# A three-stage decoder layer on one core: context logits by two 64-row halves of the PE array, the bias of Q added by PE, key maxima taken later

## The chip, the cores and the metric

The kernel runs on one core of one Trainium2 chip. The metric is device time in microseconds of one execution, as the median of several; lower is better. TensorE (PE) multiplies, VectorE (DVE), ScalarE (ACT) and GpSimd (POOL) work on what it leaves in PSUM and in SBUF, and SyncE (SP) issues most of the DMAs. Each engine takes its instructions in program order and waits on semaphores.

## The reference

The input is x of 4 batches of 1024 tokens of 256 numbers. Three layers follow one another, each with a residual sum and a layer norm. Shortened:

```python
q, k, v = x @ Wq.T + bq, x @ Wk.T + bk, x @ Wv.T + bv      # 16 heads of 16
q = softmax(q, axis=-1)                                    # over the 16 numbers of a head
k = softmax(k, axis=-2)                                    # over the 1024 tokens of a batch
state = einsum('bhnd,bhne->bhde', k, v)
x = layernorm(x + (layernorm(q @ state) * g + b) @ Wo.T + bo)
# context attention: 8 heads of 32, 77 keys, keys and values straight from the context
logits = einsum('bhqd,bhkd->bhqk', x * 32 ** -0.5, keys) + b0 - 1e30 * (1 - mask)
x = layernorm(x + softmax(logits) @ values)
# mixture of experts: 8 experts of 256 -> 1024 -> 256, the 4 best of each token
x = layernorm(x + sum over 4 experts of gate * (gelu(x @ up[e]) @ down[e]))
```

## The kernel before

The 4096 tokens are cut into 32 tiles of 128 tokens, eight to a batch. The program is a software pipeline of 52 steps, written out by hand for each engine. In step s the first part of one tile is done (`first_tile(s)`: Q, K and V), and parts of up to six older tiles (`chain_tile(s, d)`, called c0 to c6). A ninth step at the end of each batch (`closing(s)`) takes the largest K of every column, shifts and exponentiates the eight K tiles, and builds the linear attention's state. Steps 0 to 37 hold the front of the pipeline together with the splitting of the experts' weights into two float16 halves, which passes through DMA, ACT, POOL and DVE in 16 pieces. Steps 38 to 51 hold the last tiles mixed with the first expert tiles. After them only the experts are left, and a last norm.

The steps of Q, K and V. PE multiplies the turned input tile by K's and V's weights into bank 0 of a 1024-wide `big` PSUM tile (L1838) and by Q's weights into its bank 1 (L1840); as float32 each product of 128 rows is two passes. ACT copies K and V out (L1020, L1021), behind the copies of the turned tiles `x1T` and `xinT`. DVE (`take_qkv`) adds the bias to Q into SBUF (L1150, which frees Q's bank), takes the largest of each head of 16 (L1153), waits for ACT's copy of K and joins it to the running maximum `kmx` (L1159), and takes the head's maximum off Q (L1161). Then in the same step DVE divides the heads' outputs of another tile (`out_of_heads`, L1412 and L1414), takes their moments, norms the tile c4, makes the first residual sum and its moments (L1424), takes the logits' extremes (L1432, L1438), and does parts of the routing. POOL takes the square root of each variance (L827, L829), adds the constants to the residual (L835) and issues the scatters of the routing records (L851).

The context logits. `kbd` holds the context keys of a batch, negated, as a block matrix: for each half c of the 256 columns, 128 rows by 4 heads of 77 keys, in which a head's 32 rows alone are not zero. It is made by DVE (`key_blocks`, L1143) from the turned keys and the selector `hsel`. For every tile PE (`context_logits`) makes two products of 128 rows by 308 columns in float32 (L1730), one for each half c and each into its own bank, and after each adds the mask by one product of 128 rows by 308 columns in bfloat16 (L1731): `one16` has ones in row 0 alone, and row 0 of `mbf` holds the mask for 4 heads. POOL makes this row once a batch (`mask_row`, L839 and four instructions L844 of one partition each). ACT exponentiates the eight heads one by one (L992), PE turns them (L1719), and multiplies by the values (L1741).

The order in PE's queue within a step of the front: turn Z, turn Q, Q/K/V products, turn X1, turn the next input, heads' outputs (L1699), output projection (L1709), a column sum of a weight piece (L1861), turn the probabilities (L1719), context logits, turn X2, the values' products (L1741) and the router's (L1753). In the mixed steps these are set between the experts' products (`up_products` L1801, `down_products` L1820), one chunk of four after another.

Of the kernel before, what the change touches and what calls it, by code (L numbers as in the profile page):

```python
# [9 lines left out]
I32 = mybir.dt.int32  # L10
# [13 lines left out]
XPC = P // XD  # L24
KEYS = 77
# [29 lines left out]
IDENT_MADE, ONES_MADE = 2, 3  # L55
# [298 lines left out]
def layer(nc, k, rows, acc, slots, x, ctx, mask, Wq, bq, Wk, bk, Wv, bv, Wo, bo, ln_g, ln_b, xb, router, up, down, out):  # L354

    st, places = ExitStack(), ExitStack()
    with st:
# [29 lines left out]
        kbd = sb("kbd", [P, CC, XPC, KEYS])  # L387
        hsel = sb("hsel", [P, XPC])
# [4 lines left out]
        mint = sb("mint", [1, KEYS], I32)  # L393
        mrow = sb("mrow", [1, KEYS])
# [52 lines left out]
        inv = sb("inv", [P, 2 * EXP])  # L447

# [10 lines left out]
        V_extra = extra[:, C:C + CC * (P + 1)].rearrange("p (c m) -> p c m", c=CC)  # L459

# [43 lines left out]
        big_ready, qkv_taken = sem("big_ready"), sem("qkv_taken")  # L504
# [116 lines left out]
        def _(sp):  # L621
# [140 lines left out]
        def _(pool):  # L762
# [11 lines left out]
            done(pool.memset(ones[:, :], 1.0))  # L774
            done(pool.memset(V[:, :, :, P:P + 1], 1.0))
# [5 lines left out]
            done(pool.memset(one16[:, :], 0.0))  # L781
            done(pool.memset(one16[0:1, :], 1.0))
            done(pool.memset(mbf[:, :, :], 0.0))
# [8 lines left out]

            for tile, heads, d in ((hsel, XPC, XD), (bsel, HPC, LD)):
                done(pool.memset(tile[:, :], -1.0 if tile is hsel else 1.0))
                done(pool.affine_select(out=tile[:, :], in_=tile[:, :], compare_op=ALU.is_ge, fill=0.0,
                                        base=0, pattern=[[-d, heads]], channel_multiplier=1))
                done(pool.affine_select(out=tile[:, :], in_=tile[:, :], compare_op=ALU.is_ge, fill=0.0,
                                        base=d - 1, pattern=[[d, heads]], channel_multiplier=-1))
            for c in range(CC):
                done(pool.tensor_copy(state[:, c, P:P + HPC], bsel[:, :]))  # L800
# [36 lines left out]
            def mask_row(b):  # L837
                pool.wait_ge(mask_loaded, 16 * (b + 1))
# [96 lines left out]
        def _(act):  # L935
# [50 lines left out]
            def exp_logits(g):  # L986
# [4 lines left out]
                for h_ in range(XH):  # L991
                    ins = act.activation(pr[:, h_, :], logits[:, h_, :], ACT.Exp, scale=-1.0, bias=xmb[:, g % 2, h_:h_ + 1])  # L992
# [94 lines left out]
        def _(dve):  # L1087
# [3 lines left out]

            dve.wait_ge(setup_loaded2, 16 * 8)
            dve.wait_ge(consts, ONES_MADE)

            for c in range(CC):
                dve.tensor_scalar(kdiag[:, c, :], ones[:, :], gb[:, 1, c:c + 1], None, ALU.mult).then_inc(lnbb_ready, 1)
            for c in range(CC):
# [42 lines left out]
            def key_blocks(b):  # L1140
                for c in range(CC):
                    dve.wait_ge(end_ready, END_COUNT[(TB + 1) * b + TB + 2])
                    dve.tensor_tensor(kbd[:, c, :, :], turned_keys(b, c).unsqueeze(1).to_broadcast([P, XPC, KEYS]),  # L1143
                                      hsel[:, :].unsqueeze(2).to_broadcast([P, XPC, KEYS]), ALU.mult).then_inc(kt_taken, 1)

            def take_qkv(g):
                i = g % TB
                src = big_bank(("qkv", g))
                dve.wait_ge(big_ready, BIG["qkv", g] + 1)
                dve.tensor_tensor(query_tile(g), src[:, 2 * C:3 * C], bias[:, 0:C], ALU.add).then_inc(qkv_taken, 1)  # L1150
                q3 = query_tile(g).rearrange("p (h d) -> p h d", h=LH)
                dve.wait_ge(qkv_taken, g + 1)
                dve.tensor_reduce(qm[:, g % 2, :], q3, AX_X, ALU.max).then_inc(qm_ready, 1)  # L1153
# [6 lines left out]
                dve.wait_ge(qm_ready, g + 1)  # L1160
                dve.tensor_tensor(q3, q3, qm[:, g % 2, :].unsqueeze(2).to_broadcast([P, LH, LD]), ALU.subtract).then_inc(qs_ready, 1)  # L1161
# [339 lines left out]
            for s in range(MIX0):  # L1501
# [18 lines left out]
                if c1 is not None:  # L1520
# [3 lines left out]
                    moments(1, c1)  # L1524
                if piece is not None:
                    scale(piece)
# [97 lines left out]
        def _(pe):  # L1624
# [31 lines left out]
            def big_emptied(key):  # L1656
                kind, g = key
                if kind == "qkv":
                    pe.wait_ge(qkv_taken, g + 1)
# [62 lines left out]
            def context_logits(g):  # L1722
# [101 lines left out]
            for s in range(MIX0):  # L1824
# [133 lines left out]
```

## Time and profile before

| what | value |
|---|---|
| median of 3 runs | 1242.4 us (1237.84 to 1242.64) |
| the profiled execution | 1242.11 us, its span 1240.4 us |
| mean granted TensorE clock of its span | 0.938 |
| PE, DVE, POOL, ACT busy | 1080.2, 742.2, 641.0, 528.0 us |
| front of the pipeline | to about 398 us |
| mixed steps | about 398 to 567 us |
| experts alone | about 567 to 1206 us |
| last norm and stores | about 1206 us to the end |

The page gives busy times and the chain of waits: from the last instruction back to what released it, and so on to the start. A shorter instruction brings the end nearer only if it stands on this chain, and only by as much as the next chain allows. A group of instructions on one line can be partly on it. Views by windows give the stages, the timeline gives the pace of an engine. Durations of matmuls overlap in the records, so the pace is read from start to start.

### The profile page before, as it was taken

What the parts mean: (1) busy time and instruction counts of PE and PEld (TensorE: products, weight loads), DVE (VectorE), ACT (ScalarE), POOL (GpSimd) and SP (SyncE); (2) the same over time, 40 slices, a digit from 0 to 9 for tenths busy, and PEclk for the clock granted to TensorE, in tenths of its full rate; (3) what the DMA queues carried; (4) which work ended last, traced back from release to release, by engine and by line L of the source; (5) the groups of instructions that cost most, each with busy time, mean ns of one, the idle gap of its engine ahead of it and who ended that gap; (6) DMA issues with size and microseconds to landing.
All of it is one profiled execution on the core that took longest, in us unless ns stands there. A gap on an engine that the chain in (4) does not pass through costs nothing.

```text
span 1240.4 us, 27263 instructions
## 1 busy us (share of the span) xinstructions
PE 1080.2 (87%) x8576; PEld 910.7 (73%) x8576; DVE 742.2 (60%) x1813; ACT 528.0 (43%) x1148; POOL 641.0 (52%) x739
## 2 busy tenths in 40 slices
PE   6668898798864998989989999999999999999960
PEld 3345676576644887878878888888888888888750
DVE  2568988888875665765674544444444444444326
ACT  2765665544543445554433333333333333333214
POOL 3003332657665566766777555555555555554324
PEclk9878998998876998999999999999999999999985
DMA  4553222213022323334344544655444445553336
GB/s 126 167 163 96 84 81 80 51 44 84 27 63 57 81 46 67 62 66 83 47 81 74 88 78 78 78 79 78 78 79 78 75 75 75 76 75 58 63 55 247
DMA packets 159969, 100.63 MB, mean 81 GB/s; under 512 B 106956, under 2 KB 151168, under 8 KB 159840
## 3 DMA queue, kind: packets, MB, share of 16 engines
q1 hardware_dynamic: 129824, 63.21, 20.1%
q0 software_dynamic: 30016, 35.68, 19.3%
q8 instruction: 83, 1.36, 0.5%
q14 instruction: 46, 0.38, 0.1%
HBM read 49.55 MB, written 31.59 MB: 65 GB/s over the span
## 4 chain that ended last, share of the span: by engine, by line
PE 67%; DVE 12%; ACT 8%; issue 4%; DMA 4%; POOL 4%; SPq 1%; DVEq 0%; ACTq 0%; POOLq 0%
PE big L1801 28%; PE big L1820 15%; PE trans L1820 11%; PE big L1838 2%; POOL slot_records L851 2%; ACT pr L992 1%; PE big L1730 1%; PE small L1709 1%; PE trans L1632 1%; PE small L1741 1%; PE small L1887 1%; DMA w_down<-in_L_ffn_down_w_dram 1%; DVE stat L1130 1%; PE big L1840 1%; ACT L992 1%
## 5 line engine op out<-in xcount | busy, mean ns | idle before, releaser
L1801 PE MATMUL big<-xgT,w_up 128*128 128x256 f16 (+1 forms) x3456 | 410.7, 268 | 10.7 <-ACT h L976 6.2
L976 ACT ACTIVATE h<-big,up_scale 128x512 f32<-128x512 f32 x270 | 185.6, 687 | 438.0 <-PE big L1801 429.2
L1801 PEld LDWEIGHTS big<-xgT,w_up 128*128 x3456 | 326.3, 99 | 54.3 <-issue 14.3
L881 POOL DMA_INDIRECT token_sums<-y,rec x135 | 223.4, 1654 | 246.6 <-ACT y L984 216.8
L1404 DVE TENSOR_SCALAR hh<-h,h_scale 128x512 f16<-128x512 f32 x270 | 133.1, 493 | 346.7 <-ACT h L976 346.1
L1820 PE MATMUL big<-w_down,hh 128*128 x1312 | 223.7, 272 | 2.5 <-DVE hl L1406 2.2
L1406 DVE SCALAR_TENSOR_TENSOR hl<-h,h_scale,hh 128x512 f16<-128x512 f32 x270 | 203.3, 753 | 9.7
L1820 PE MATMUL big<-w_down,hl 128*128 x656 | 178.8, 273 | 0.0
L866 POOL DMA_INDIRECT xg<-token_rows,rec x135 | 136.5, 1011 | 51.3 <-issue 39.0
L851 POOL DMA_INDIRECT slot_records<-recs,posi x128 | 133.2, 1040 | 34.8 <-issue 34.8
L1820 PE MATMUL trans<-w_down,hh 128*128 x848 | 144.6, 273 | 2.3 <-DVE hl L1406 2.3
L827 POOL TENSOR_SCALAR ve<-mv 128x1 f32<-128x1 f32 x96 | 27.3, 284 | 229.3 <-DVE mv L1134 228.7
L1820 PEld LDWEIGHTS big<-w_down,hh 128*128 128x128 f16 x1312 | 128.2, 98 | 20.8 <-issue 4.5
L1820 PE MATMUL trans<-w_down,hl 128*128 x424 | 115.6, 273 | 0.0
L1820 PEld LDWEIGHTS trans<-w_down,hh 128*128 128x128 f16 x848 | 82.9, 98 | 12.6 <-issue 2.6
L1838 PE MATMUL big<-wqkv_XA,xinT 128*128 128x512 f32 x128 | 72.1, 693 | 1.4 <-ACT xinT L944 1.4
L1820 PEld LDWEIGHTS big<-w_down,hl 128*128 128x128 f16 x656 | 64.1, 98 | 7.3
L829 POOL TENSOR_TENSOR rstd<-ve,nhalf 128x1 f32<-128x1 f32 x96 | 60.4, 629 | 8.0
L992 ACT ACTIVATE pr<-big,xmb 128x77 f32<-128x77 f32 x256 | 58.8, 348 | 11.3 <-DVE xmb L1438 11.1
L951 ACT ACTIVATE pT<-trans 128x512 f32<-128x512 f32 x64 | 24.5, 434 | 60.2 <-PE trans L1719 59.4
L1709 PE MATMUL small<-woT,zT 128*128 128x256 f32 x128 | 40.6, 447 | 10.9 <-DVE L L1470 4.2
L1730 PE MATMUL big<-kbd,x1T 128*128 128x308 f32 x128 | 45.9, 449 | 0.0
(261 smaller groups left out, 1416.1 us busy)
## 6 DMA issues: line engine op xcount, KB each, us to landing
w_down<-in_L_ffn_up_w_dram SPq DMA_DIRECT2D x8, 1024.0 KB, 5.0
w_down<-in_L_ffn_down_w_dram SPq DMA_DIRECT2D x7, 1024.0 KB, 5.7
wqkv_XA<-in_x_dram SPq DMA_DIRECT2D x32, 128.0 KB, 2.7
XRES<-in_x_dram SPq DMA_DIRECT2D x32, 128.0 KB
token_sums<-X SPq DMA_DIRECT2D x32, 128.0 KB, 1.7
token_rows<-XR SPq DMA_DIRECT2D x32, 128.0 KB, 1.7
sums<-token_sums SPq DMA_DIRECT2D x8, 512.0 KB, 6.5
out_dram<-sums SPq DMA_DIRECT2D x8, 512.0 KB, 2.6
```

The source lines that it names most:

```text
L829: pool.tensor_tensor(rstd[:, kind, at:at + 1], ve[:, kind, at:at + 1], nhalf[:, 0:1], ALU.pow).then_inc(rstd_ready[kind], 1)
L851: pool.indirect_dma_start(slots, bass.IndirectOffsetOnAxis(ap=posi[:, half, e:e + 1], axis=0), recs[:, half, e // TOPK, e % TOPK, :], None ...
L866: pool.indirect_dma_start(xg[:, t % 2, j, :], None, rows[0:EARLY_BATCHES * N, :] if t < EARLY else rows, bass.IndirectOffsetOnAxis(ap=rec[ ...
L881: pool.indirect_dma_start(acc[0:EARLY_BATCHES * N, :] if t < EARLY else acc, bass.IndirectOffsetOnAxis(ap=rec[:, t % RING, j, 0:1], axis=0 ...
L976: act.activation(h[:, i % H_RING, :], psu[up_bank(i)], ACT.Gelu_apprx_tanh, scale=k["up_scale"][:, t:t + 1]).then_inc(gelu_ready, 1)
L992: ins = act.activation(pr[:, h_, :], logits[:, h_, :], ACT.Exp, scale=-1.0, bias=xmb[:, g % 2, h_:h_ + 1])
L1404: dve.tensor_scalar(hh[:, i % HALF_RING, :], h[:, i % H_RING, :], k["h_scale"][:, t:t + 1], None, ALU.mult).then_inc(hh_ready, 1)
L1406: dve.scalar_tensor_tensor(out=hl[:, i % HALF_RING, :], in0=h[:, i % H_RING, :], scalar=k["h_scale"][:, t:t + 1], in1=hh[:, i % HALF_RING, :],
L1730: pe.matmul(dst, x1T[:, c, :], kbd[:, c, :, :].rearrange("p h k -> p (h k)"), start=True, stop=False)
L1801: ins = pe.matmul(psu[up_bank(i)][:, j * size(t):(j + 1) * size(t)], w[:, ws, c, m:m + P], xgT[:, t % 2, xs * CC + c, 0:size(t)], start=(n ...
L1820: ins = pe.matmul(ytile(t)[:, j, :], (hh, hl)[hs][:, i % HALF_RING, at:at + P], w[:, ws, c, :], start=(c == 0 and j == 0 and hs == 0 and w ...
L1838: pe.matmul(dst[:, 0:2 * C], xT[:, c, :], wqkv[:, c, C:3 * C], start=(c == 0), stop=(c == CC - 1))
```

## The change

- `kbd` keeps 2 heads of 77 keys for each half c in place of 4: rows 0 to 63 hold two heads and rows 64 to 127 the other two, in the same columns. `hsel` gets two more columns for it.
- PE makes the logits in six products of 64 rows: two in bfloat16 for the mask (308 columns each), which now come first, and four in float32 of 154 columns. Products of rows 0 to 63 go into one bank and those of rows 64 to 127 into the other. The order of heads in PSUM changes, and ACT writes them back in the old order.
- `one16` has ones everywhere; `mint`, `mrow` and `mbf` have 128 rows, of which 0 and 64 carry the mask and the others zeros. POOL makes `mbf` in one instruction in place of four; SP loads the mask twice.
- Q's bias is added by PE: one bfloat16 product of 128 rows by 256 columns before the products of Q, with the bias as a sum of three bfloat16 rows. DVE makes these rows at the start in eight instructions, before it takes the `cv` sums.
- DVE takes the heads' maxima and the differences of Q straight from PSUM; the addition is gone, and Q's bank is free after the differences.
- The running maximum of K is taken later in the step, after the moments of the first residual sum (`take_key`).

```diff
-        kbd = sb("kbd", [P, CC, XPC, KEYS])
+        kbd = sb("kbd", [P, CC, HALF_HEADS, KEYS])
...
+                else:
+                    sp.wait_ge(consts, CONST_STEPS)
                 sp.dma_start(ctx_sb[:, :], ctx[b, :, 0:C]).then_inc(ctx_loaded, 16)
-                sp.dma_start(mint[:, :], mask[b:b + 1, :]).then_inc(mask_loaded, 16)
+                for a in range(2):
+                    sp.dma_start(mint[a * HALF_ROWS:a * HALF_ROWS + 1, :], mask[b:b + 1, :]).then_inc(mask_loaded, 16)
...
-                for h in range(XPC):
-                    ins = pool.tensor_scalar(mbf[0:1, h, :], mrow[:, :], -MASKED, None, ALU.mult)
-                ins.then_inc(mask_ready, 1)
+                pool.tensor_scalar(mbf[:, :, :], mrow[:, :].unsqueeze(1).to_broadcast([P, XPC, KEYS]), -MASKED, None, ALU.mult).then_inc(mask_ready, 1)
...
+            def query_bias_rows():
+
+                high, low = XR[:, 0, 0:C].bitcast(BF16), XR[:, 1, 0:C].bitcast(BF16)
+                left, rest = X2[:, 0, :], X2[:, 1, :]
+                dve.memset(bq_rows[:, :], 0.0).then_inc(bq_step, 1)
+                dve.tensor_copy(high, bias[:, 0:C]).then_inc(bq_step, 1)
+                dve.wait_ge(bq_step, 2)
+                dve.tensor_tensor(left, bias[:, 0:C], high, ALU.subtract).then_inc(bq_step, 1)
+                dve.wait_ge(bq_step, 3)
+                dve.tensor_copy(low, left).then_inc(bq_step, 1)
+                dve.wait_ge(bq_step, 4)
+                dve.tensor_tensor(rest, left, low, ALU.subtract).then_inc(bq_step, 1)
+                dve.wait_ge(bq_step, 5)
+                dve.tensor_copy(bq_rows[0:1, :], bias[0:1, 0:C]).then_inc(bq_ready, 1)
+                dve.tensor_copy(bq_rows[32:33, :], left[32:33, :]).then_inc(bq_ready, 1)
+                dve.tensor_copy(bq_rows[64:65, :], rest[64:65, :]).then_inc(bq_ready, 1)
...
-                src = big_bank(("qkv", g))
+                src = big_bank(("qkv", g))[:, 2 * C:3 * C].rearrange("p (h d) -> p h d", h=LH)
                 dve.wait_ge(big_ready, BIG["qkv", g] + 1)
-                dve.tensor_tensor(query_tile(g), src[:, 2 * C:3 * C], bias[:, 0:C], ALU.add).then_inc(qkv_taken, 1)
-                q3 = query_tile(g).rearrange("p (h d) -> p h d", h=LH)
-                dve.wait_ge(qkv_taken, g + 1)
-                dve.tensor_reduce(qm[:, g % 2, :], q3, AX_X, ALU.max).then_inc(qm_ready, 1)
+                dve.tensor_reduce(qm[:, g % 2, :], src, AX_X, ALU.max).then_inc(qm_ready, 1)
+                dve.wait_ge(qm_ready, g + 1)
+                dve.tensor_tensor(query_tile(g).rearrange("p (h d) -> p h d", h=LH), src,
+                                  qm[:, g % 2, :].unsqueeze(2).to_broadcast([P, LH, LD]), ALU.subtract).then_inc(qs_ready, 1)
+
+            def take_key(g):
+                i = g % TB
                 dve.wait_ge(kv_ready, 2 * g + 1)
...
-                dve.wait_ge(qm_ready, g + 1)
-                dve.tensor_tensor(q3, q3, qm[:, g % 2, :].unsqueeze(2).to_broadcast([P, LH, LD]), ALU.subtract).then_inc(qs_ready, 1)
...
                     moments(1, c1)
+                if a is not None:
+                    take_key(a)
...
                 logits = big_into(("lg", g))
+                for a in range(2):
+                    at = LOGIT0 + a * XPC * KEYS
+                    pe.matmul(logits[:, at:at + XPC * KEYS], one16[row_half(a), :], mbf[row_half(a), :, :].rearrange("p h k -> p (h k)"),
+                              start=True, stop=False, skip_group_check=True)
                 for c in range(CC):
-                    dst = logits[:, LOGIT0 + c * XPC * KEYS:LOGIT0 + (c + 1) * XPC * KEYS]
-                    pe.matmul(dst, x1T[:, c, :], kbd[:, c, :, :].rearrange("p h k -> p (h k)"), start=True, stop=False)
-                    ins = pe.matmul(dst, one16[:, :], mbf[:, :, :].rearrange("p h k -> p (h k)"), start=False, stop=True)
+                    for a in range(2):
+                        at = LOGIT0 + (CC * a + c) * HALF_HEADS * KEYS
+                        ins = pe.matmul(logits[:, at:at + HALF_HEADS * KEYS], x1T[row_half(a), c, :], kbd[row_half(a), c, :, :].rearrange("p h k -> p (h k)"),
+                                        start=False, stop=(c == CC - 1), skip_group_check=True)
...
+                    if a == 0:
+                        pe.wait_ge(consts, ONE16_MADE)
+                        pe.wait_ge(bq_ready, 3)
+                    pe.matmul(dst[:, 2 * C:3 * C], one16[:, :], bq_rows[:, :], start=True, stop=False)
                     for c in range(CC):
-                        ins = pe.matmul(dst[:, 2 * C:3 * C], xT[:, c, :], wqkv[:, c, 0:C], start=(c == 0), stop=(c == CC - 1))
+                        ins = pe.matmul(dst[:, 2 * C:3 * C], xT[:, c, :], wqkv[:, c, 0:C], start=False, stop=(c == CC - 1))
```

## Rows read from the trace of the kernel before

**Rows 1.** The page: the engines' busy times, the chain's lines.
```profile
PE 1080.2 (87%) x8576; PEld 910.7 (73%) x8576; DVE 742.2 (60%) x1813; ACT 528.0 (43%) x1148; POOL 641.0 (52%) x739
...
PE big L1801 28%; PE big L1820 15%; PE trans L1820 11%; PE big L1838 2%; POOL slot_records L851 2%; ACT pr L992 1%; PE big L1730 1%; PE small L1709 1%; PE trans L1632 1%; PE small L1741 1%; PE small L1887 1%; DMA w_down<-in_L_ffn_down_w_dram 1%; DVE stat L1130 1%; PE big L1840 1%; ACT L992 1%
```

**Rows 2.** Windows by stage: from:to, length, busy time per engine, granted clock.
```profile
85.00:180.00 95.00, 81.78 (x445) 61.50 (x444) 79.44 (x225) 61.15 (x168) 32.69 (x63) 0.93 0.30 95
...
340.00:398.00 58.00, 30.72 (x170) 25.48 (x167) 37.87 (x121) 21.09 (x64) 35.87 (x46) 0.72 0.20 53
398.00:567.00 169.00, 152.56 (x1237) 132.11 (x1237) 110.79 (x286) 87.73 (x199) 110.86 (x126) 0.95 0.34 66
```

**Rows 3.** The chain, 268 to 345 us: start, length, engine, line.
```profile
283.04 0.43 POOL mbf L844
...
285.18 0.24 POOL ve L827
...
290.11 3.41 PE big L1838 x4
293.52 1.17 PE big L1840 x4
...
328.99 1.03 PE big L1730 x2
```

**Rows 4.** The same chain, one step that waits for K.
```profile
310.88 1.72 PE big L1838 x4
312.59 0.86 PE big L1840 x4
...
314.26 0.40 ACT K L1020
314.68 0.43 DVE kmx L1159
315.11 0.33 DVE Q L1161
315.44 0.18 DVE rden L1412
```

**Rows 5.** The same chain, one step in which DVE itself is late.
```profile
304.22 0.34 DVE Q L1150
...
304.92 0.41 DVE kmx L1159
305.34 0.34 DVE Q L1161
305.67 0.18 DVE rden L1412
```

**Rows 6.** The chain, 460 to 500 us: one mixed step.
```profile
477.34 1.31 PE big L1801 x12
478.65 0.52 PE big L1730 x2
479.17 0.13 PE big L1731
479.31 0.52 PE big L1730 x2
479.82 0.13 PE big L1731
...
481.26 1.06 PE small L1741 x10
```

**Rows 7.** Timeline of PE, 465 to 500 us: the record's own length.
```profile
478.49 0.68 PE L1730 MATMUL big<-kbd,x1T 128*128 128x308 f32 x2
```

**Rows 8.** Timeline of the start: DVE before and at the second cv sum.
```profile
13.37 0.48 DVE L1096 TENSOR_SCALAR kdiag<-ones,gb 128x128 f32<-128x128 f32 x2 [13.37 <-DMA rw<-in_L_ffn_router_w_dram]
...
16.08 0.29 DVE L1099 TENSOR_TENSOR cvec<-small,cvec 128x128 f32<-128x128 f32 x1 [0.56 <-PE small L1685]
```

**Rows 9.** Groups by line and shape, 30 to 490 us: a copy on DVE.
```profile
L1156 DVE COPY kmx<-K 128x256 f32<-128x256 f32 x2 | 0.6, 288 | 0.0
```

More of the change, by code:

```diff
@@ L24 @@
 XPC = P // XD
+HALF_ROWS, HALF_HEADS = P // 2, XPC // 2
 KEYS = 77
@@ L54 @@
 CONST_STEPS = 32 + 3 * FCH + TOPK + EXP
-IDENT_MADE, ONES_MADE = 2, 3
+IDENT_MADE, ONES_MADE, ONE16_MADE = 2, 3, 4
 PIECES = 4
@@ L386, in layer @@
         x2T = sb("x2T", [P, CC, P])
-        kbd = sb("kbd", [P, CC, XPC, KEYS])
-        hsel = sb("hsel", [P, XPC])
+        kbd = sb("kbd", [P, CC, HALF_HEADS, KEYS])
+        hsel = sb("hsel", [P, XPC + HALF_HEADS])
         bsel = sb("bsel", [P, HPC])
@@ L392, in layer @@
         vx = sb("vx", [P, FCH, SPAN_MAX, XD + 1])
-        mint = sb("mint", [1, KEYS], I32)
-        mrow = sb("mrow", [1, KEYS])
+        mint = sb("mint", [P, KEYS], I32)
+        mrow = sb("mrow", [P, KEYS])
         mbf = sb("mbf", [P, XPC, KEYS], BF16)
@@ L447, in layer @@
         inv = sb("inv", [P, 2 * EXP])
+        bq_rows = sb("bq_rows", [P, C], BF16)
         trans = [ps(f"trans{i}", [P, 4, P]) for i in range(2)]
@@ L459, in layer, with row_half, head_at @@
         V_extra = extra[:, C:C + CC * (P + 1)].rearrange("p (c m) -> p c m", c=CC)
+        def row_half(a):
+            return slice(a * HALF_ROWS, (a + 1) * HALF_ROWS)
+        def head_at(n):
+            a, c, j = n // XPC, n // HALF_HEADS % CC, n % HALF_HEADS
+            return XPC * c + HALF_HEADS * a + j
         def key_tile(g):
@@ L503, in layer @@
         rt_taken, pos_taken, early_taken = sem("rt_taken"), sem("pos_taken"), sem("early_taken")
-        big_ready, qkv_taken = sem("big_ready"), sem("qkv_taken")
+        big_ready, bq_step, bq_ready = sem("big_ready"), sem("bq_step"), sem("bq_ready")
         lnbb_ready, woT_gained, woT_centred = sem("lnbb_ready"), sem("woT_gained"), sem("woT_centred")
@@ L774, in _ @@
             done(pool.memset(ones[:, :], 1.0))
+            done(pool.memset(one16[:, :], 1.0))
             done(pool.memset(V[:, :, :, P:P + 1], 1.0))
@@ L780, in _ @@
             done(pool.memset(nhalf[:, :], -0.5))
-            done(pool.memset(one16[:, :], 0.0))
-            done(pool.memset(one16[0:1, :], 1.0))
-            done(pool.memset(mbf[:, :, :], 0.0))
+            done(pool.memset(mint[:, :], 1))
             done(pool.memset(vx[:, :, :, :], 0.0))
@@ L791, in _ @@
                                         pattern=[[KEYS, h1 - h0]], channel_multiplier=-1))
-            for tile, heads, d in ((hsel, XPC, XD), (bsel, HPC, LD)):
-                done(pool.memset(tile[:, :], -1.0 if tile is hsel else 1.0))
-                done(pool.affine_select(out=tile[:, :], in_=tile[:, :], compare_op=ALU.is_ge, fill=0.0,
+            for tile, heads, d, value in ((hsel[:, 0:XPC], XPC, XD, -1.0), (bsel[:, :], HPC, LD, 1.0)):
+                done(pool.memset(tile, value))
+                done(pool.affine_select(out=tile, in_=tile, compare_op=ALU.is_ge, fill=0.0,
                                         base=0, pattern=[[-d, heads]], channel_multiplier=1))
-                done(pool.affine_select(out=tile[:, :], in_=tile[:, :], compare_op=ALU.is_ge, fill=0.0,
+                done(pool.affine_select(out=tile, in_=tile, compare_op=ALU.is_ge, fill=0.0,
                                         base=d - 1, pattern=[[d, heads]], channel_multiplier=-1))
+            done(pool.tensor_tensor(hsel[:, XPC:XPC + HALF_HEADS], hsel[:, 0:HALF_HEADS], hsel[:, HALF_HEADS:XPC], ALU.add))
             for c in range(CC):
@@ L837, in mask_row @@
             def mask_row(b):
-                pool.wait_ge(mask_loaded, 16 * (b + 1))
+                pool.wait_ge(mask_loaded, 16 * 2 * (b + 1))
                 pool.tensor_scalar(mrow[:, :], mint[:, :], -1.0, 1.0, ALU.mult, ALU.add).then_inc(mask_step, 1)
@@ L990, in exp_logits @@
                 logits = big_bank(("lg", g))[:, LOGIT0:LOGIT0 + XH * KEYS].rearrange("p (h k) -> p h k", h=XH)
-                for h_ in range(XH):
-                    ins = act.activation(pr[:, h_, :], logits[:, h_, :], ACT.Exp, scale=-1.0, bias=xmb[:, g % 2, h_:h_ + 1])
+                for n in range(XH):
+                    ins = act.activation(pr[:, head_at(n), :], logits[:, n, :], ACT.Exp, scale=-1.0, bias=xmb[:, g % 2, n:n + 1])
                 ins.then_inc(p_ready, 1)
@@ L1096, in _ @@
                 dve.tensor_scalar(kdiag[:, c, :], ones[:, :], gb[:, 1, c:c + 1], None, ALU.mult).then_inc(lnbb_ready, 1)
+            query_bias_rows()
             for c in range(CC):
@@ L1658, in big_emptied @@
                 if kind == "qkv":
-                    pe.wait_ge(qkv_taken, g + 1)
+                    pe.wait_ge(qs_ready, g + 1)
                     pe.wait_ge(kv_ready, 2 * (g + 1))
```

4 lines of the change are left out of this document (2 added, 2 removed).

## Prediction, made before the change was run

> **What bounds the kernel now.** I read the page first [rows 1]. PE is busy for 87% of the span and most of the chain is PE's, but nearly all of that is experts' work on L1801 and L1820, which the change leaves alone. The windows say where there is something to win [rows 2]. In the front of the pipeline (85 to 180 us) PE is busy 81.8 of 95 us and DVE 79.4: neither is the bound alone, and the chain passes from one to the other. From 340 to 398 us PE is half idle. In the mixed steps (398 to 567 us) PE is busy 152.6 of 169 us. Then I followed the chain itself through the front and the mixed steps, and counted in which steps the touched lines stand on it.
>
> The Q/K/V products L1838 stand on it in 12 of 32 tiles (2.1% of the span, about 26 us, as the page has it [rows 1]); three of the 12 run at the lower clock, 3.41 us in place of 1.72 [rows 3, 4]. The running maximum of K stands on it in 19 tiles. In 14 of them it comes behind ACT's copy of K [rows 4]: Q's products end at 313.46 and DVE divides the heads' outputs (rden) at 315.44, 2.0 us later, though nothing in rden needs K. In five DVE is late by itself, and the four operations follow one another without a gap [rows 5]. The context logits stand on the chain in 7 tiles of the front and in all 8 of the mixed steps [rows 6]. The row of the mask stands on it once [rows 3].
>
> **The change part by part.** Minus is a gain.
>
> *Maxima of Q and K.* In a step that waits for K, DVE goes on after Q's products with the reduction (the record of each of the four operations is about 0.42 us) and the difference, some 0.85 us in all by the spacing of [rows 5]: reduction 0.45, difference 0.33, small gaps. The heads' outputs, which PE makes behind two turns, are ready about 1.1 us after Q's products. So rden starts 1.1 us after them in place of 1.7 to 2.0: 0.6 to 0.9 earlier. The maximum of K is still to be taken, 0.35 us, but later; where the chain stays on DVE up to there this is given back. I take 0.55 a tile between 0.25 and 0.85: 14 tiles, -7.7 us (-3.5 to -11.9). In the five steps of [rows 5] one operation of about 0.33 us goes: 304.22 to 305.67 is 1.45, and becomes 1.1 with K's maximum counted: -1.7 us. Q's bank is freed by the second operation as before, counted from PE's end 0.4 us later; the next product into it comes a step later (some 10 us), so this costs nothing. The K maximum of the last tile of a batch, for which PE's turn in the closing step waits, moves about 2 us back within its own step, before left products of the next, and is hidden by them.
>
> *Bias by PE.* One product of 256 columns in bfloat16 is added to each tile. Twelve float16 products of 256 columns take 1.31 us [rows 6], so it is 0.11 us, or 0.22 at the lower clock. On the chain in 12 tiles, three of them slow: +1.6 us. In the other tiles PE isn't late.
>
> *Context logits.* Before: 478.65 to 479.95, 1.30 us [rows 6]: four passes of 0.26 in float32 and two masks of 0.13. After: eight float32 passes of 154 columns and two masks. If each pair of halves runs together, that is 8 x 0.13 / 2 + 0.13 = 0.64 us. If none does, it is 8 x 0.13 + 2 x 0.13 = 1.30. The trace has no product of 64 rows and no change of the rows used, so its cost is bounded: 0, or the tail of a product that is normally hidden, 0.68 - 0.52 = 0.16 us [rows 6, 7], once going in and once coming out. The bounds are 0.64 and 1.62. Between them a row decides: ten float32 passes of at most 99 columns take 1.06 us (L1741 [rows 6]), 0.106 each although their columns need but 0.08, so a pass doesn't get shorter than about 0.106, the load of its weights. Eight such and two masks at half price are 0.98; with some loss at the changes I take 1.10, a gain of 0.2 (0.66 gained to 0.32 lost). With 15 tiles on the chain: -3.0 us (-9.9 to +4.8).
>
> What speaks against this part stands in the Trainium skill too. TensorEngine Tiling (Array Packing), Key Properties, says that changing the tiling mode drains TensorE; this kernel would change it twice a tile. No row here shows a drain; by it the value goes to the upper end. TensorE: Matmul & The Clock Gate, LDWEIGHTS (loading the stationary operand), has the load take as long as its columns at 1.2 GHz whatever the rows, an estimate of 8 x 107 ns = 0.85 us for the eight; the pace of L1741 agrees.
>
> *Mask, keys, setup.* On POOL four instructions (283.04 to 285.18, 2.14 us [rows 3]) become one of 128 x 308. Its price isn't in the trace: it lies between 0.4 (one of the four) and about 1.2 (by its columns from the 0.8 us of a 128 x 256 addition there); I take 0.7, and -1.4 us, for it is on the chain once. `key_blocks` halves its columns: two operations of 0.47 become about 0.3; on the chain in one batch, -0.3. SP issues one more small DMA a batch (0.4 us), with the tile's stores behind it in SP's queue; nothing on the chain waits for these; if something did, +1.6. At the start DVE makes the bias rows in eight operations: about 0.29 for each of five copies [rows 9], 0.42 for each of two differences, a memset, in all some 2.6 us from 13.9 to 16.5, ahead of the two cv sums, of which DVE took the second at 16.08 [rows 8]. Both now come after 16.5, so the first qkv product comes about 0.7 later; since step 0 of DVE is shorter after that, the weights' first load comes 0.6 later. +0.6 (0 to +1.3).
>
> Sum: -7.7 - 1.7 + 1.6 - 3.0 - 1.4 - 0.3 + 0.6 = -11.9 us. What is late next takes part of it: ACT, whose copies of K, X1 and the input keep their times, and POOL, which is busy 35.9 of the 58 us between 340 and 398, more than PE [rows 2], and whose scatters there only move with their start. I take 2 us off: -10. The profiled execution took 1242.1 and the median is 1242.4, so they may be taken as one: 1232 us.
>
> **The rivals.** *The halves don't run together* (the change doesn't do what it says): 1.60 a tile with the changes of rows, +4.5 in place of -3.0: 1239.5. For it: both passes of a half follow each other in program order, so neighbours are of different halves only every second time. Against it: they go into different banks and rows. *The halves run together fully*: 0.64 a tile, -9.9 in place of -3.0: 1225. Against it: the pace of 0.106 a pass. *The wait for K only moves*: the heads' outputs aren't ready earlier, or K's maximum comes to a point where DVE is just as late. Then of 9.4 us about 3 is left: 1238.5. For it: PE's turn of X1 and the input stand before the heads' outputs, and DVE is 84% busy in the front. *Slower: PE's clock falls in more of the front's steps.* It stands at 0.93 there [rows 2] with 86% of PE busy. A slow step costs about 1.7 us in L1838, 0.5 to 0.8 in L1840, 1.3 in the logits (two passes take 1.03 in place of 0.52 [rows 3, 6]) and 0.8 in L1741, about 4.5 in all where PE is on the chain. Two more such steps than now eat the whole gain, four give 1232 + 18 = 1250. For it: work is taken off PE where the clock already falls at times. Against it: it is less than a tenth of PE's work in a step.
>
> **How the numbers follow.** The sum as told has 0.40, with a range of its own of 1227 to 1237; no concurrency 0.20, full concurrency 0.15, the wait only moves 0.15, the clock 0.10. The range of 1222 to 1246 takes in the first four and their bounds, and leaves out most of the fifth. A difference under about 0.5% (6.2 us) can't be told from none here. Below 1236.2 fall nine tenths of the first case, all of the third, a fifth of the second and the fourth: 0.58. Above 1248.6 falls most of the fifth: 0.08. Between them 0.34.
>
> **What would show it.** Right: rden about 1.1 us behind the end of L1840 in the steps of the second kind of chain; the six logits' products from first start to the next product's start in 1.0 to 1.2 us; expert work of the last stage unchanged and the first mixed step starting 8 to 9 us earlier than at about 398; a mixed step shorter by 0.2 us. Wrong: the logits over 1.3 us; an ACT or POOL wait in front of the same steps with the same length of the front; a granted clock below 0.9 between 85 and 340 us. If DVE is still on the chain at K's maximum, in its new place, the first term was too large.

## The result, and the profile after

The changed kernel takes 1221.6 us (median of 4 runs, 1219.7 to 1223.5) against 1240.1 of the kernel before beside it; the ratio is 0.9856, with a 95% interval of 0.9831 to 0.9882. That is 18 us faster, where 10 were forecast, and just outside the range. (The forecast of 1232 started from 1242.4 us; 2.3 of the 10.4 us between it and the measured 1221.6 are the lower starting point of this comparison, the other 8 are the gain.) Two more comparisons on other chips gave 0.9837 (0.981 to 0.9864) and 0.985 (0.9825 to 0.9874), so 18 to 20 us. The runs of the kernel before spread more (1231.5 to 1243.8 in 29 runs on one chip) than those of the changed one, and its profiled execution of 1242.1 lies at the slow end. So what a part is worth is told from the timed ratios, in microseconds of 1238, and the traces tell where.

The page of the changed kernel, the busy times and the chain by engine (the busy times of before are in [rows 1]):

```profile
PE 1064.8 (87%) x8736; PEld 898.6 (74%) x8736; DVE 729.8 (60%) x1789; ACT 527.4 (43%) x1148; POOL 637.1 (52%) x727
...
PE 63%; DVE 15%; ACT 7%; POOL 6%; issue 5%; DMA 4%; SPq 1%; DVEq 0%; ACTq 0%; POOLq 0%
```

The chain by engine of the kernel before:

```profile
PE 67%; DVE 12%; ACT 8%; issue 4%; DMA 4%; POOL 4%; SPq 1%; DVEq 0%; ACTq 0%; POOLq 0%
```

PE's share of the whole chain is down from 67% to 63% and DVE's is up from 12% to 15%. The windows, in the same columns as [rows 2], the later ones shifted with the stages:

```profile
85.00:180.00 95.00, 83.16 (x520) 63.26 (x519) 82.80 (x236) 66.27 (x185) 32.54 (x66) 0.94 0.32 101
...
340.00:380.00 40.00, 21.13 (x115) 18.21 (x115) 21.57 (x69) 16.13 (x44) 26.97 (x31) 0.67 0.16 37
380.00:550.00 170.00, 153.81 (x1334) 134.57 (x1333) 111.50 (x286) 88.11 (x199) 113.63 (x125) 0.97 0.36 68
```

DVE is busy 82.8 of the 95 us from 85 to 180, against 79.4 in [rows 2], although each tile has one operation less: more tiles fall into the same 95 us. Where the time went can be read from the first starts of the last Q/K/V product, of the first expert product and of the last logits, before and after. PE's timelines, before:

```profile
334.30 1.88 PE L1838 MATMUL big<-wqkv_XA,xinT 128*128 128x512 f32 x4
...
550.38 0.68 PE L1730 MATMUL big<-kbd,x1T 128*128 128x308 f32 x2
```

and after:

```profile
315.63 1.88 PE L1875 MATMUL big<-wqkv_XA,xinT 128*128 128x512 f32 x4
...
379.69 2.53 PE L1838 MATMUL big<-xgT,w_up 128*128 128x256 f16 x11 [3.27 <-DMA xgT<-xg]
...
526.76 0.31 PE L1762 MATMUL big<-mbf,one 64*128 64x308 bf16 x2
```

In these two executions 18.7 us are won by the end of the front (334.3 to 315.6), the same 18.7 are there when the experts begin (398.4 in the chain of before, 379.7 after), and 4.9 more come in the mixed steps (550.4 to 526.8 is 23.6). So most of it lies in the front and the rest in the mixed steps. (This pair overstates the front, for the trace of before is of a slow execution; three traces of the changed kernel have the first expert product at 378.8, 379.7 and 380.6.)

A piece of the chain after, from 85 to 150 us (start, length, engine and line). It stands on DVE from one tile's Q to the next, where before it passed through PE and ACT [rows 4]:

```profile
125.08 0.32 DVE qm L1179
125.42 0.42 DVE Q L1181
125.84 0.17 DVE rden L1442
126.04 0.44 DVE Z L1444
...
127.44 0.41 DVE X L1454
...
128.43 0.41 DVE kmx L1191
...
134.72 0.32 DVE qm L1179
```

How often DVE waited for the Q products of PE is in the waits between 17 and 340 us (who waited for whom: us in total, times, longest), before and after:

```profile
DVE Q L1150 <- PE big L1840: 16.0, 12, 3.6
```

```profile
DVE qm L1179 <- PE big L1881: 13.8, 9, 3.5
```

In the kernel before DVE waited for them in 12 of 32 tiles. In the other 20 it came to them from earlier work of its own, in 17 of these over 0.8 us after PE had finished them, so DVE was late already. (Some of that work had itself waited for ACT's pieces of the weights.) In the changed kernel DVE came without a wait in 23 tiles.

### The profile page after: what moved, and what is told of

The parts are those of the page before. It is cut to its first block, busy times and chain, and to the rows that moved or that the text cites. A ratio compares the mean times of both kernels' runs of the same rounds, so it can differ in the third digit from the quotient of the medians.

```text
span 1217.7 us, 27552 instructions
## 1 busy us (share of the span) xinstructions
PE 1064.8 (87%) x8736; PEld 898.6 (74%) x8736; DVE 729.8 (60%) x1789; ACT 527.4 (43%) x1148; POOL 637.1 (52%) x727
## 3 DMA queue, kind: packets, MB, share of 16 engines
q0 software_dynamic: 30016, 35.68, 20.2%
## 4 chain that ended last, share of the span: by engine, by line
PE 63%; DVE 15%; ACT 7%; POOL 6%; issue 5%; DMA 4%; SPq 1%; DVEq 0%; ACTq 0%; POOLq 0%
PE big L1838 29%; PE big L1857 15%; PE trans L1857 11%; POOL slot_records L862 3%; DMA w_down<-in_L_ffn_down_w_dram 1%; DVE stat L1159 1%; ACT pr L1003 1%; PE small L1741 1%; DVE w_down L1155 1%; DVE xm L1462 1%; PE small L1778 1%; ACT L1003 1%; PE trans L1664 1%; ACT L987 1%; PE big L1875 1%
## 5 line engine op out<-in xcount | busy, mean ns | idle before, releaser
L1838 PE MATMUL big<-xgT,w_up 128*128 128x256 f16 (+1 forms) x3456 | 411.2, 268 | 11.2 <-ACT h L987 6.2
L1838 PEld LDWEIGHTS big<-xgT,w_up 128*128 x3456 | 326.5, 99 | 55.2 <-issue 14.7
L1875 PE MATMUL big<-wqkv_XA,xinT 128*128 128x512 f32 x128 | 69.6, 671 | 1.4 <-ACT xinT L955 1.4
L1664 PE MATMUL trans<-ident,X 128*128 128x128 f32 x128 | 27.7, 300 | 22.5 <-DVE X L1167 11.1
```

What stands on the lines that cost most here:

```text
L1838: ins = pe.matmul(psu[up_bank(i)][:, j * size(t):(j + 1) * size(t)], w[:, ws, c, m:m + P], xgT[:, t % 2, xs * CC + c, 0:size(t)], start=(n ...
```

## Experiments: the three parts, alone and in pairs

The change falls into the logits in halves (L, with the mask in one instruction), the bias on PE (B) and the later maximum of K (K). All six mixtures were timed. The edits take parts of the diff back; the core of each:

```diff
# without L: products of 128 rows, kbd of 4 heads, mask row by four instructions
-                for c in range(CC):
-                    for a in range(2):
-                        at = LOGIT0 + (CC * a + c) * HALF_HEADS * KEYS
...
+                    pe.matmul(dst, x1T[:, c, :], kbd[:, c, :, :].rearrange("p h k -> p (h k)"), start=True, stop=False)
+                    ins = pe.matmul(dst, one16[:, :], mbf[:, :, :].rearrange("p h k -> p (h k)"), start=False, stop=True)
# without B: DVE adds the bias
-                    pe.matmul(dst[:, 2 * C:3 * C], one16[:, :], bq_rows[:, :], start=True, stop=False)
+                dve.tensor_tensor(query_tile(g), big_bank(("qkv", g))[:, 2 * C:3 * C], bias[:, 0:C], ALU.add).then_inc(qkv_taken, 1)
# without K: the maximum between the heads' maxima and the differences
+                take_key(g)
                 dve.wait_ge(qm_ready, g + 1)
```

L alone (l_only):

> Only the logits by 64-row halves (with the mask row in one POOL instruction); Q's bias and the maximum of K stay where they were. In the changed kernel a tile's logits take 0.76 us on PE in place of 1.30. Theory A (the parts are worth what their places on the chain say and add up): 15 tiles x 0.54 = 8.1 us, and 1 us for the mask: about 9 us faster than before. Theory B (PE and DVE share a loop; while DVE still waits for K behind PE, a shorter PE shows up fully in the mixed steps alone): 8 x 0.54 = 4.3 us there, and 2 to 3 in the front: 6 to 7 us.

K alone (k_only):

> Only the running maximum of K is taken later; the bias stays on DVE and the logits are of 128 rows. Theory A: in the 14 tiles in which DVE waited for ACT's copy of K the wait goes, 0.25 to 0.5 us each net of the maximum itself: 4 to 7 us faster. Theory B (the wait for K was what tied DVE to PE and ACT, with ACT's exponentials ahead of the copy): 8 to 12 us faster, most of it between 90 and 200 us.

B alone (b_only):

> Only Q's bias goes to PE; K's maximum stays between the heads' maxima and the differences. (The bias rows lie in memory of scale tables that are free by then, for there is no room beside the wide key blocks.) Theory A: in the steps in which DVE is late one operation of 0.33 us goes (5 tiles, 1.7 us), on PE 0.11 is added on 12 tiles (1.6 us), and the eight operations at the start cost up to 0.6: 0 to 1 us slower or no change. Theory B (DVE's load is what counts everywhere): 32 x 0.33 = 10 us faster at most, 4 or more.

B and K (b_k):

> Bias on PE and K's maximum later, logits of 128 rows as before. Theory A: the sum of the two alone, 4 to 8 us faster. Theory B: more than the sum, 10 to 12 us, since only with both is DVE free to go on right behind PE; then the logits' halves add 7 to 9 on top.

L and K (l_k):

> The changed kernel with Q's bias back on DVE: K's maximum late and the logits in halves stay. Theory C: the bias addition costs DVE 0.33 to 0.4 in most of the 32 tiles: 7 to 11 us slower than the changed kernel. Theory A: 1 us faster to 1 us slower, since PE's product and the rows at the start go away too.

L and B (l_b):

> The changed kernel with K's maximum back between the heads' maxima and the differences. If DVE's work were all that counts, nothing would change, since the same operation is only moved. If the wait for ACT's copy of K is a cost of its own (12.0 us of such waits in the trace with the bias on PE alone, against 5.4 before), it is 8 to 14 us slower than the changed kernel.

The whole change again, beside them (after_again):

> The changed kernel once more, beside runs of the kernel before on the same chip as the three kernels sent with it. Every theory: 16 to 20 us faster than before.

| parts | median us | ratio to before (95%) | us |
|---|---|---|---|
| L | 1235.0 | 0.9981 (0.996 to 1.0002) | -2.4 |
| K | 1229.4 | 0.9947 (0.9927 to 0.9967) | -6.6 |
| B | 1233.7 | 0.9975 (0.9951 to 0.9999) | -3.1 |
| B, K | 1222.0 | 0.9878 (0.985 to 0.9906) | -15.1 |
| L, K | 1227.9 | 0.9906 (0.9877 to 0.9934) | -11.6 |
| L, B | 1233.0 | 0.9949 (0.9928 to 0.9969) | -6.3 |
| all | 1219.3 | 0.9837 (0.981 to 0.9864) | -20.2 |

B and K alone make 9.7, together 15.1. The 5.4 us between them are beyond the spread (the means of the four kernels' runs on that chip give 4.5, give or take 3). B is worth 3.1 by itself and 8.5 once K's maximum is out of the way (8.6 beside L and K, on another chip); K is worth 6.6 by itself and 12 beside B, and 12 to 14 beside L and B. The waits of DVE between 17 and 340 us say why (the columns as above). Before, then with B alone, then with all:

```profile
DVE kmx L1159 <- ACT K L1020: 5.4, 10, 1.6
```

```profile
DVE kmx L1195 <- ACT K L1034: 12.0, 18, 2.1
```

```profile
DVE kmx L1191 <- ACT K L1031: 0.9, 2, 0.6
```

Take the addition off DVE and it comes sooner to the maximum of K, where it waits for ACT's copy: 12.0 us in 18 tiles in place of 5.4 in 10. What was taken off is given back as a wait. With the maximum moved the wait is gone. L and B together show the same wait without the move, 11.8 us in 18 tiles. Theory A of the expectations holds for K alone (6.6 in 4 to 7). B alone, at 3.1, lies between the two theories. For the pair more than the sum was right, as theory B has it, and 15.1 is more than its 10 to 12.

L is the surprise of the other kind: 2.4 us alone, where both theories had 6 to 9 and the interval reaches from a gain of 5 to no change; 3.2 on top of B, 5.0 on top of K, and between 3 and 5 on top of both.

The mixed steps alone can account for that. From the first expert product to the product behind the last logits it is 153.3 us before, 153.2, 150.4 and 151.2 with B, with K and with both, and 147.8 to 148.3 in the six traces that have L (L, L and B, L and K, and three of the whole change): 2 to 5.5 us less. In the front nothing of L is left over.

One thing goes with it that the experiments did not separate. Each kernel with L ran at a lower granted clock, averaged over the span and all its runs, than its partner without: 0.937 for L against 0.942 before, 0.937 for L and B against 0.945 for B, 0.941 for L and K against 0.946 for K, 0.942 for all against 0.949 for B and K. Among the 29 runs of the kernel before on one chip a clock lower by 0.001 goes with a time longer by 0.9 us. If the same held between kernels, the lower clock would take back 4 to 7 us of what L gives, an estimate that no run tests.

## Experiments: do the halves run together?

Edits of the changed kernel: all six products over 128 rows (each then takes the rows of both halves, so that kernel doesn't compute the layer); and the order of the four float32 products. The first edit, its lines shortened:

```diff
-                    pe.matmul(logits[:, at:at + XPC * KEYS], one16[row_half(a), :], mbf[row_half(a), :, :]
+                    pe.matmul(logits[:, at:at + XPC * KEYS], one16[:, :], mbf[:, :, :]
...
-  x1T[row_half(a), c, :], kbd[row_half(a), c, :, :]
+  x1T[:, c, :], kbd[:, c, :, :]
```

```diff
-                for c in range(CC):
-                    for a in range(2):
+                for a in range(2):
+                    for c in range(CC):
```

> The changed kernel with every one of the six logits' products over all 128 rows, the number of products, their columns and their banks as they are (the logits are wrong, as each product takes both halves' rows; the masks are added twice). Halves at once: the six take 0.76 us in the changed kernel and 8 x 0.13 + 2 x 0.13 = 1.30 here, 0.54 more in each of the 8 mixed steps, and 4 to 6 us in all. If the 0.76 came from fewer columns or from the masks standing first, the six take 0.76 here too and the time is the same.

> The changed kernel with the four float32 products in the order half 0, half 0, half 1, half 1. If only neighbours in the queue run together, two of eight passes overlap and the six products take about 1.1 us in place of 0.76, 2 to 4 us slower in all. If PE looks further ahead, nothing changes.

PE's timelines between 445 and 500 us, from the twelve expert products ahead to the next one behind; a record of several is from the first start to the last modelled end. All over 128 rows:

```profile
458.52 1.47 PE L1838 MATMUL big<-xgT,w_up 128*128 128x256 f16 x12
459.83 0.42 PE L1762 MATMUL big<-mbf,one 128*128 128x308 bf16 x2
460.09 1.21 PE L1767 MATMUL big<-kbd,x1T 128*128 128x154 f32 x8
461.14 0.38 PE L1857 MATMUL big<-w_down,hh 128*128 x2
```

The halves, in the order of the change:

```profile
455.20 1.47 PE L1838 MATMUL big<-xgT,w_up 128*128 128x256 f16 x12
456.61 0.31 PE L1762 MATMUL big<-mbf,one 64*128 64x308 bf16 x2
456.75 0.69 PE L1767 MATMUL big<-kbd,x1T 64*128 64x154 f32 x8
457.37 0.39 PE L1857 MATMUL big<-w_down,hh 128*128 x2
457.60 0.27 PE L1857 MATMUL big<-w_down,hl 128*128 x1
```

The halves one after the other:

```profile
456.26 0.30 PE L1762 MATMUL big<-mbf,one 64*128 64x308 bf16 x2
456.40 0.80 PE L1767 MATMUL big<-kbd,x1T 64*128 64x154 f32 x8
457.12 0.39 PE L1857 MATMUL big<-w_down,hh 128*128 x2
```

From the first mask product to the next expert product it is 1.31, 0.76 and 0.86 us. The same products over all rows take what the old ones took (1.30, [rows 6]), so the 0.55 comes from the halves running together and not from fewer columns or from the order of the masks.

Not all of it is a gain. The twelve expert products ahead take 1.31 us to the next start when that product has 128 rows (459.83 - 458.52, and 1.31 in [rows 6]), and 1.41 when it has 64 (456.61 - 455.20; 1.40 or 1.41 in the four such steps between 430 and 500 us). So going over to 64 rows costs 0.10 us. Coming back costs about 0.01: 0.23 us from 457.37 to 457.60, where the kernel before has 0.22. With the entry a tile's logits cost PE 0.86 us in place of 1.31, a gain of 0.45, or 3.6 us in the 8 mixed steps.

With one half after the other it costs 0.10 more, less than the 0.3 expected of strict neighbours. In time, rows128 has a ratio of 0.9863 (1222.2 us) and order_by_half 0.9856 (1220.7), against 0.9837 and 0.985 of the changed kernel on other chips. For rows128 that is 2 to 3 us, hardly beyond the spread (4 to 6 were expected), and for the order nothing that can be measured. The mixed stretch of rows128 takes 153.3 us, as before the change, and its first expert product starts at 379.8 us, as in the changed kernel. So the longer logits cost the front nothing that shows. Here too the clock stands beside it: rows128 ran at 0.946 on average, the changed kernel at 0.942, so it isn't shown whether the front would gain from shorter logits at an equal clock.

## Experiments: which engine sets the front's pace?

Doses of work were put on one engine. On DVE, at the early place, with a semaphore of its own:

```diff
+                dve.tensor_reduce(qm[:, g % 2, :], src, AX_X, ALU.max).then_inc(twice, 1)
+                dve.wait_ge(twice, g + 1)
                 dve.tensor_reduce(qm[:, g % 2, :], src, AX_X, ALU.max).then_inc(qm_ready, 1)
```

> The changed kernel, with the reduction of the heads' maxima done twice for every tile of Q (some 0.42 us and a wait more on DVE, 32 times, at the place where the bias addition stood). Theory C (in the front DVE's own work sets the pace almost everywhere once K's wait is gone): 32 x 0.42 x 0.7 or more, 9 to 13 us slower than the changed kernel. Theory A (as in the forecast, DVE is late in few steps): 2 to 5 us slower.

> The kernel before, with the same reduction done twice ahead of the maximum of K. Theory C: there part of the steps hide it behind ACT's copy of K, so it costs less than in the changed kernel, 3 to 7 us. If it costs as much as in the changed kernel (9 to 13), DVE set the pace before as well, and the forecast's five tiles were miscounted.

The same on `kmx` at the late place, and the early one again beside it:

```diff
+                    dve.tensor_tensor(kmx[:, :], kmx[:, :], key_tile(g), ALU.max).then_inc(twice, 1)
+                    dve.wait_ge(twice, g - g // TB)
                     dve.tensor_tensor(kmx[:, :], kmx[:, :], key_tile(g), ALU.max).then_inc(kmx_ready, 1)
```

> The changed kernel with the running maximum of K done twice, in its late place behind the moments of the first residual sum: 28 operations of 0.35 to 0.42 us and a wait more on DVE. Theory D (what counts is where on DVE an operation stands: ahead of the heads' outputs it delays every engine, behind the moments only DVE's own tail): 2 to 5 us slower than the changed kernel, as the mirror image of the 3.6 us that taking them out gave. Theory C (DVE's load alone): 28/32 of the doubled reduction, 9 to 10 us slower.

> The changed kernel with the reduction of the heads' maxima done twice, beside the doubled maximum of K on the same chip. Both theories: 9 to 12 us slower than the changed kernel, that is 7 to 10 us faster than the kernel before.

Load taken off DVE, and load put on PE, beside the changed kernel on the same chip:

```diff
-                if a is not None:
+                if a is not None and a % TB == 0:
                     take_key(a)
```

```diff
+                    for n_ in range(4):
+                        pe.matmul(dst[:, 2 * C:3 * C], one16[:, :], bq_rows[:, :], start=True, stop=(n_ < 3))
```

> The changed kernel again, beside the three others on one chip. Every theory: 16 to 20 us faster than before.

> The changed kernel without the running maximum of K but for the first tile of each batch: 28 operations of some 0.35 us leave DVE (K is shifted by the first tile's maxima, which the softmax cancels, though it no longer guards against overflow). Theory C, DVE's load sets the pace of the front: the slope of the doubled reduction, 0.7 to 0.8 of each operation, gives 28 x 0.35 x 0.75 = 7 us faster than the changed kernel. If the chain has gone over to PE and POOL by then: 0 to 3 us.

> The changed kernel with the bias product of 256 columns done four times for every tile of Q: 3 x 0.11 = 0.33 us more on PE in 32 tiles of the front, 10.6 us of PE work. If PE were on the front's path as in the forecast (12 of 32 tiles): 4 us slower. If DVE sets the pace: 0 to 2 us, and then the bias on PE was nearly free and so were the logits' halves in the front.

| kernel | median us | ratio to before (95%) | against the changed kernel |
|---|---|---|---|
| before, heads' maxima twice | 1249.9 | 1.0083 (1.0055 to 1.011) | (before: +10.3) |
| changed, heads' maxima twice | 1230.1 | 0.9926 (0.9897 to 0.9956) | +11.0 |
| the same, other chip | 1228.7 | 0.9928 (0.9911 to 0.9945) | +9.7 |
| changed, K's maximum twice, late | 1228.5 | 0.993 (0.9911 to 0.9948) | +9.9 |
| changed, K's maximum in 4 tiles alone | 1216.8 | 0.9822 (0.9796 to 0.9847) | -3.5 |
| changed, bias product four times | 1219.7 | 0.9852 (0.9815 to 0.9889) | +0.2 |
| changed | 1220.4 | 0.985 (0.9825 to 0.9874) | |

(Each in microseconds of 1238, from the ratio of the changed kernel on the same chip, or, for the two at 0.9928 and 0.993, from 0.985.)

A DVE operation of 0.42 us and a wait, 32 times, is about 14.4 us, and costs 10 to 11: some 0.7 of it in the changed kernel. Late in the step the doubled maximum costs as much (9.9 for 28 operations). Theory D, that the place counts, falls; theory C, that DVE's load sets the pace, holds for load that is added.

In the kernel before the dose costs 10.3 us too, with an interval of 6.8 to 13.6, or 0.5 to 0.9 of its length. Theory C had 3 to 7 there, so its idea that the wait for K hides much of it failed, and by that expectation's own words DVE set the pace before as well. Two cautions go with the figure. The eleven runs reach from 1242.5 to 1254.4 us, and the trace is of the fastest; in it the experts start at 401.1 us, only 2.7 later than before, so no trace shows where the 10 us arise. And those runs had a mean clock of 0.936 against 0.942 of the kernel before beside them, so a part of the price may be PE's lower clock. How much isn't shown.

Going the other way, 28 operations (about 10 us) taken off give 3.5. Six runs of each on one chip, 1215.4 to 1220.2 us and 1218.4 to 1222.6, make it 3 us, give or take 2.3: a gain, but less than the 7 that the slope gave. So something else comes close behind DVE. On PE, 10.6 us more work in the same steps cost +0.2. The interval of about 4.5 us either way would still hold the 4 us of the forecast's view; the trace speaks against them, for its first expert product starts at 379.3 us, within the 378.8 to 380.6 of the changed kernel. Which engine comes next, ACT, POOL or the loop through all of them, wasn't settled.

Two versions try whether the place of the maximum can give more: at the end of DVE's step (behind the norm of X1), with the bias rows made at the start where DVE waits for PE; and the same without the last tile of a batch.

```diff
-                if a is not None:
-                    take_key(a)
...
                     norm(1, c1, X1[:, c1 % 3, :], x1_ready)
+                if a is not None:
+                    take_key(a)
                 routing(s)
```

> The changed kernel with K's maximum at the end of DVE's step, behind the logits' extremes and the norm of X1, and the eight operations on the bias rows moved behind the gain of the output weights, where DVE waits 2.2 us for PE. If moving work away from what PE and ACT wait for is worth more than DVE's load: 1 to 4 us faster than the changed kernel. If DVE's load alone is left: 0.5 us faster (the start) or no change.

> The changed kernel with the bias rows made where DVE waits for PE at the start, and K's maximum at the end of DVE's step except in a batch's last tile, where it stays, since PE waited 7 us for it in the trace in which all had been moved. If where DVE's work stands counts beside how much it is: 2 to 5 us faster than the changed kernel. If only its amount counts: 0.5 us.

They took 1216.9 us (0.9839, 0.9809 to 0.9869) and 1220.1 us (0.9845, 0.9821 to 0.987). Neither can be told from the changed kernel (0.9837, 0.985), so the 2 to 5 us expected of the second did not come. In the first one's trace PE waits 7.7 us in three closing steps between 85 and 340 us for the maximum of K:

```profile
PEld small L1887 <- DVE kmx L1191: 7.7, 3, 3.9
```

## Why the prediction was wrong, step by step

- *What bounds the kernel now.* This is the step that failed: the count that DVE is late by itself in five tiles, and with it the -1.7 us for the work taken off DVE. The count was made on the chain, and a chain names one engine at a time. The waits in the same trace show that DVE waited for the Q products in only 12 of 32 tiles and was late by over 0.8 us in 17 of the others. The doubled reduction in the kernel before costs 0.5 to 0.9 of its length, where five of 32 tiles would be 0.16. "Neither is the bound alone" was too mild. A step in which the chain passes through ACT's copy of K looks like a step that DVE doesn't bound; but in [rows 4] everything from kmx on is DVE again, and the wait for K is short beside the work that follows.
- *Maxima of Q and K, steps with a wait.* Forecast -7.7 (3.5 to 11.9), measured for K's move alone -6.6. The mechanism and the size held: the trace of before has 5.4 us of such waits, and that of the changed kernel 0.9. The sign named in advance came as well: where DVE waited for Q's products between 85 and 340 us, rden starts 1.0 to 1.1 us behind them in the changed kernel and 1.8 to 2.1 before.
- *The bias addition taken off DVE.* Forecast -1.7 from five tiles and +1.6 for PE, so about nothing, with the 0.6 at the start against it. Measured with K moved: -8.5, or 0.27 us in each of 32 tiles. This term of the sum was mis-sized, by 7 to 8 us, and is most of the error. It could be bounded from [rows 5]: 0.33 in each of 32 tiles is 10.6 at most, a bound that the range should have taken in.
- *Bias by PE.* Forecast +1.6 for 12 tiles on the chain. Three times that work more cost +0.2, give or take 4.5, and did not move the start of the experts in the trace. So it was covered as far as these runs can tell, and L1838's place on the chain in 12 tiles did not make PE's length a price there.
- *Logits.* The size of one was wrong: 0.86 us with the way in, in place of the 1.10 taken, so 0.45 gained a tile and not 0.2. A pass was taken to be no shorter than 0.106, the load of its weights; eight passes in 457.37 - 456.75 = 0.62 us make 0.078. Either loads of different rows overlap as well or a load of 64 rows is shorter; the runs don't separate the two. The count was wrong the other way: of 15 tiles the 8 mixed ones paid (2 to 5.5 us between the traces without and with the halves), and the 7 of the front next to nothing. 15 x 0.2 = 3.0 came out near the measured 2.4 to 5.0 by two errors that cancel, which is luck.
- *The drain.* TensorEngine Tiling (Array Packing), Key Properties, in the Trainium skill says that changing the mode drains TensorE. The traces show a cost of that kind, 0.10 us going in and about 0.01 coming out; the forecast's bound was 0 to 0.16 each way. That the 0.10 is a drain isn't shown. The same section says that tiles can load weights and multiply in parallel, and the 0.078 us a pass agrees. TensorE: Matmul & The Clock Gate, LDWEIGHTS (loading the stationary operand), in the Trainium skill has the load go by its columns and not by its rows, an estimate of 107 ns for 128 columns; the eight passes of halves took 0.62 us and not 0.85, so the figure is no floor for a sum over both halves.
- *Mask, keys, start.* The one POOL instruction takes 1.01 us, inside the bounds of 0.4 to 1.2 and above the 0.7 taken; `key_blocks` takes 0.306 an operation, as forecast. The rows of the bias took DVE 2.5 us (13.49 to 15.99), and the first cv sum came at 16.02, as worked out; the two kernels that made them later, and took K's maximum later too, could not be told from the changed one.
- *What is late next.* 2 us were taken off for it. No run tests it for the change itself; behind the change 3 to 3.5 were gained of 10 taken off.

Of the rivals, that the halves don't run together is refuted by the pace (0.76 against 1.31), that the wait only moves is refuted for the change as a whole but is just what happens with the bias alone (12.0 us of waits), and the granted clock between 85 and 340 us is 0.92 before and after (0.90 and 0.93 in the two later traces), so the clock's rival didn't come as told; the lower mean clock of every kernel with L is its weaker form, and what that costs isn't shown. Full concurrency was the nearest, with 1225, and would still have been 3 us too slow, for it shared the error in DVE's term.

## What to carry to other kernels

Where the chain of waits alternates between engines, count what stands on it, but count also in how many steps each engine waits for the other: here the 12 of 32 in the trace of before show that DVE was late in more than half. Then test an engine's weight by a dose: one operation more for each tile, which changes no result, tells in one run how much of added work counts. It doesn't tell what work taken off would give (3 to 3.5 us of 10 here); that takes a dose the other way. Look at the granted clock of both kernels beside it. An edit that takes work off such an engine is worth little while the engine runs into a wait behind another one, and the edit that moves the wait is worth more beside it; cost such a pair together, not as two counts. And a matmul's place on the chain need not be a price: a few tenths of a microsecond more of PE's work a tile changed nothing here that could be measured.

## What the runs showed of the hardware

- Two products of 64 rows in different halves of the array and different banks run together in float32 too: eight passes of 154 columns in 0.62 us, 0.078 each, against 0.131 each over 128 rows ((461.14 - 460.09) / 8).
- Going over from products of 128 rows to products of 64 cost 0.10 us (1.41 in place of 1.31 ahead of the first of them), and coming back about 0.01.
- The halves need not be strict neighbours in the queue: with both products of a half one after the other, the eight passes take 0.72 us in place of 0.62.
